# State-space stage of an adaLN network: merged dt weights, a new order of the small steps, softplus summed by TensorE

## The reference, cut to what matters

```
xz = u @ m_in_w.T ; xc, z = split(xz)                  # 256 channels each
xc = silu(causal_conv4(xc) + conv_b)
x_dbl = xc @ xproj_w.T                                  # 8 dt ranks, 16 B, 16 C
dt = softplus(x_dbl[:8] @ dt_w.T + dt_b)
h  = exp(dt * A) * h + dt * B * xc                      # scan over 512 tokens, 16 states
y  = (sum over states of h * C + xc * Dp) * silu(z)
out = y @ m_out_w.T
```

## Time and profile before

| | before |
|---|---|
| median of 3 runs | 2072.83 us |
| profiled execution, its own time | 2059.48 us |
| its span | 2057.8 us |
| mean granted TensorE clock | 0.837 |
| busy: TensorE, VectorE, ScalarE, GpSimd | 80%, 66%, 49%, 48% of the span |

### The profile page before, as it was taken

How to read it: one execution, slowest core, us unless ns; L and a number is a source line. 1 busy time by engine, 2 the same in 40 slices (tenths; PEclk the granted TensorE clock), 3 DMA queues, 4 the chain that set the end, 5 groups by cost and what they waited for, 6 DMA issues and landing times. The chain is left out here.

```text
span 2057.8 us, 23202 instructions
## 1 busy us (share of the span) xinstructions
PE 1652.5 (80%) x7221; PEld 730.4 (35%) x7221; DVE 1350.7 (66%) x1527; ACT 1003.5 (49%) x1638; POOL 995.8 (48%) x524
## 2 busy tenths in 40 slices
PE   7767788888888888875855957698888889879998
PEld 5221222222222222211454744354444445633333
DVE  3079999999999999999552123566565655384444
ACT  3566666676666776674122523154444445441111
POOL 1169999999999999998441153011111000040000
PEclk8878888888888888877957966599999989989999
DMA  3044344434443433333003221422233330100001
GB/s 140 2 104 104 92 103 103 103 93 103 103 103 95 101 90 88 89 87 91 16 30 103 82 67 50 116 59 56 49 77 79 79 79 4 46 0 0 0 0 41
DMA packets 78636, 145.41 MB, mean 71 GB/s; under 512 B 10214, under 2 KB 40782, under 8 KB 76854
## 3 DMA queue, kind: packets, MB, share of 16 engines
q1 hardware_dynamic: 75350, 134.98, 25.8%
q0 software_dynamic: 3216, 9.51, 1.4%
HBM read 87.27 MB, written 23.53 MB: 54 GB/s over the span
## 5 line engine op out<-in xcount | busy, mean ns | idle before, releaser
L574 POOL TENSOR_TENSOR PR<-H,CS 128x1024 f32<-128x1024 f32 x256 | 599.4, 2359 | 75.1 <-DVE H L550 52.8
L550 DVE TENSOR_TENSOR_SCAN H<-DA,X 128x1024 f32<-128x1024 f32 x192 | 431.1, 2273 | 0.0
L456 PE MATMUL psY<-PR,fold 128*64 128x512 f32 x1024 | 341.0, 766 | 4.9 <-POOL PR L574 4.9
L538 DVE TENSOR_TENSOR X<-DU,psB 128x1024 f32<-128x1024 f32 x192 | 235.8, 1228 | 72.9 <-DMA DU<-ab 56.8
L526 ACT ACTIVATE DA<-DT,negA 128x511 f32<-128x511 f32 x384 | 247.6, 709 | 7.3 <-DMA DT<-W 6.4
L1278 ACT ACTIVATE a_PT<-a_psS 128x512 f32<-128x512 f32 x320 | 181.3, 601 | 138.5 <-PE a_psS L1182 134.6
L1325 DVE TENSOR_REDUCE a_MX<-a_psM 128x1 f32<-128x384 f32 (+3 forms) x352 | 205.0, 635 | 47.0 <-PE a_psM L1197 45.5
L1196 PE MATMUL a_psM<-a_kst,a_qst 72*128 72x512 bf16 (+3 forms) x512 | 147.4, 336 | 28.0 <-DMA a_kst<-scratch_k 17.5
L550 DVE TENSOR_TENSOR_SCAN H<-X,XS 128x1024 f32<-128x1024 f32 x64 | 146.2, 2284 | 30.2 <-ACT X L526 30.2
L585 POOL TENSOR_TENSOR XS<-DU,BS 128x1024 f32<-128x1024 f32 x64 | 151.0, 2360 | 0.0
L436 PE MATMUL psB<-ST,sel 96*128 96x512 bf16 x128 | 60.8, 475 | 106.4 <-DVE X L538 106.4
(11 more groups left out here) (258 smaller groups left out, 2733.0 us busy)
## 6 DMA issues: line engine op xcount, KB each, us to landing
CS<-c_rows SPq DMA_DIRECT2D x128, 256.0 KB, 3.8
DT<-W SPq DMA_DIRECT2D x64, 256.0 KB, 4.3
DU<-ab SPq DMA_DIRECT2D x64, 256.0 KB, 4.4
BS<-c_rows SPq DMA_DIRECT2D x64, 256.0 KB, 5.3
scratch_q<-a_partsq SPq DMA_DIRECT2D x24, 384.0 KB, 3.4
a_qst<-scratch_q SPq DMA_DIRECT2D x8, 1152.0 KB
a_kst<-scratch_k SPq DMA_DIRECT2D x24, 384.0 KB
scratch_k<-a_partsk SPq DMA_DIRECT2D x8, 384.0 KB, 4.4
```

What stands on the lines that cost most here:

```text
L456: last = nc.tensor.matmul(psY[h * HP:(h + 1) * HP, n % 2 * T:(n % 2 + 1) * T], fold[:, :], chunk(PR[n % 4], h), start=False, stop=n >= NS - 2)
L538: nc.vector.tensor_tensor(both(X[s % 2][:, :]), DU[p][:, at:at + 2, :], psB[:, :].unsqueeze(1).to_broadcast([P, 2, T]), ALU.mult).then_inc ...
L550: nc.vector.tensor_tensor_scan(H[s % 4][:, :], decay, x, 0.0, ALU.mult, ALU.add).then_inc(scan_done, 1)
L574: nc.gpsimd.tensor_tensor(both(PR[s % 4][:, :]), both(H[s % 4][:, :]), CS[q % 2][:, s // 2 % 2, :].unsqueeze(1).to_broadcast([P, 2, T]), A ...
```

## The change

The dt weights are merged once, in the input stage: the 8 columns of the x-projection that give dt's ranks are multiplied by dt_w, so that dt is made straight from u (dtW, 128 rows, two chunks). To that end the input stage begins with two transposes, a VectorE copy and two products on TensorE, and a second VectorE copy. In the turn, d0 and d1 come first, then new steps s0 and s1 (the sum rl + ab by products with the identity, copied to rl by ScalarE), then xp, n1 and n2, and c0 to c1 and z0, z1 last. Exp and Ln become entries of the table (slots 5 and 6). GpSimd no longer adds, and multiplies by u in its slot 11. The queue sends DT ahead of the store to c_rows. In the prologue SiLU is made in two halves. In the attention stage the queue stores the parts of q and k before it sends the first half of the maxima. Context lines far from a change are left out.

```diff
...
+def dt_weights(W):
+
+    at = OFF1["wmod0"][0] + NCH * T
+    return W[:, at:at + NCH * NCH * P].rearrange("p (c m) -> p c m", c=NCH)
+
+
 def mamba_inputs_stage(nc, W, hT, XP, convW, diagD, sel, fold, nsel):
...
+    dtW = dt_weights(W)
...
         ps = [ctx.enter_context(nc.psum_tensor(f"xp_ps{i}", [P, T], F32)) for i in range(4)]
+        xprojT = ctx.enter_context(nc.sbuf_tensor("xprojT", [104, NCH * P], F32))
+        dt_ps = ctx.enter_context(nc.psum_tensor("dt_ps", [P, NCH * P], F32))
+        dtW_ps = ctx.enter_context(nc.psum_tensor("dtW_ps", [P, NCH, NCH * P], F32))
         sem = lambda name: ctx.enter_context(nc.semaphore(name))
-        xp_ps_ready, xp_done = sem("xp_ps_ready"), sem("xp_done")
+        xp_ps_ready, xp_done, dtW_step = sem("xp_ps_ready"), sem("xp_done"), sem("dtW_step")
         with nc.Block() as block:
+            @block.vector
+            def _(dve):
+                dve.wait_ge(dtW_step, 1)
+                nc.vector.tensor_copy(xprojT[:, :], dt_ps[0:104, :]).then_inc(dtW_step, 1)
+                dve.wait_ge(dtW_step, 3)
+                nc.vector.tensor_copy(dtW[:, :, :], dtW_ps[:, :, :])
+
             @block.tensor
             def _(pe):
+                for c in range(NCH):
+                    last = nc.tensor.transpose(dt_ps[0:104, c * P:(c + 1) * P], w("xproj")[:, c * 104:(c + 1) * 104], w("ident"))
+                last.then_inc(dtW_step, 1)
+                pe.wait_ge(dtW_step, 2)
+                for c in range(NCH):
+                    last = nc.tensor.matmul(dtW_ps[:, c, :], xprojT[96:104, c * P:(c + 1) * P], w("dt_w")[96:104, :], start=True, stop=True)
+                last.then_inc(dtW_step, 1)
                 with pe.Fori(0, B // 2) as i:
...
         UZ = [sb(f"UZ{i}", [P, 4 * T]) for i in range(2)]
-        xd = W[:, OFF1["wmod0"][0] + NCH * T:OFF1["wmod0"][0] + 3 * T]
+        xd = W[0:2 * NS, OFF1["conv_w"][0]:OFF1["conv_w"][0] + T]
+        dtW = dt_weights(W)
         ST = [sb(f"ST{i}", [96, T], BF16) for i in range(2)]
...
         ASIDE = (3, 7, 11, 15)
-        ORDER = ("mout", "xp", "n1", "n2", "d0", "d1", "c0", "c1", "z0", "z1")
-        FIRST = ("c0", "c1", "z0", "z1", "xp", "n1", "n2", "d0", "d1", "c0+", "c1+", "z0+", "z1+")
+        ORDER = ("mout", "d0", "d1", "s0", "s1", "xp", "n1", "n2", "c0", "c1", "z0", "z1")
+        FIRST = ("c0", "c1", "d0", "d1", "s0", "s1", "xp", "n1", "n2", "z0", "z1", "c0+", "c1+", "z0+", "z1+")
         BEFORE, EACH = len(FIRST), len(ORDER)
...
-        PE_AT = {3: ("mout",), 4: ("xp",), 5: ("n1",), 6: ("n2",), 7: ("d0",), 8: ("d1",),
-                 10: ("c0a",), 11: ("c0b",), 13: ("c1a",), 14: ("c1b",), 16: ("z0",), 17: ("z1",)}
-        ACT_AT = {3: ("silu", "mout"), 4: ("xp",), 5: ("n1",), 6: ("n2",), 7: ("d0",), 8: ("d1",), 12: ("c0",), 15: ("c1",), 16: ("z0",), 17: ("z1",)}
+        PE_AT = {3: ("mout",), 4: ("d0",), 5: ("d1",), 7: ("s0",), 8: ("s1",), 9: ("xp",), 10: ("n1",), 11: ("n2",),
+                 12: ("c0a",), 13: ("c0b",), 14: ("c1a",), 15: ("c1b",), 16: ("z0",), 17: ("z1",)}
+        ACT_AT = {3: ("silu", "mout"), 4: ("d0",), 5: ("d1", "exp"), 6: ("ln",), 7: ("s0",), 8: ("s1",), 9: ("xp",), 10: ("n1",), 11: ("n2",),
+                  13: ("c0",), 15: ("c1",), 16: ("z0",), 17: ("z1",)}
...
             elif k == "xp":
-                pe.wait_ge(silu_done, v + 1)
                 for c in range(NCH):
...
                 n = int(k[1])
-                last = nc.tensor.matmul(pp[:, :], w("dt_w")[96:104, n * P:(n + 1) * P], xd[96:104, :], start=True, stop=True)
+                if k == "d0":
+                    pe.wait_ge(silu_done, v + 2 if u is not None else 1)
+                if k == "s0":
+                    pe.wait_ge(softplus_step, 2 * v + 2)
+                for c in range(NCH):
+                    if k[0] == "d":
+                        last = nc.tensor.matmul(pp[:, :], dtW[:, c, n * P:(n + 1) * P], chunk(UZ[pv], c), start=c == 0, stop=c == NCH - 1)
+                    else:
+                        last = nc.tensor.matmul(pp[:, :], w("ident"), chunk((rl, ab)[c], n), start=c == 0, stop=c == NCH - 1)
             last.then_inc(pp_ready, 1)
...
-                act.wait_ge(pp_copied, EACH * u + BEFORE if u is not None else used(None, "z1") + 1)
-                if u is not None:
-                    act.wait_ge(fin_done, u + 1)
+                act.wait_ge(pp_copied, EACH * u + BEFORE)
+                act.wait_ge(fin_done, u + 1)
                 nc.scalar.activation(UZ[pv][:, :], pre[:, :], ACT.Silu).then_inc(silu_done, 1)
+                return
+            if k == "silu_u":
+
+                act.wait_ge(pp_copied, used(None, "c1") + 1)
+                nc.scalar.activation(UZ[0][:, 0:NCH * T], pre[:, 0:NCH * T], ACT.Silu).then_inc(silu_done, 1)
+                return
+            if k == "silu_z":
+
+                act.wait_ge(pp_copied, used(None, "z1") + 1)
+                nc.scalar.activation(UZ[0][:, NCH * T:], pre[:, NCH * T:], ACT.Silu).then_inc(silu_done, 1)
+                return
+            if k == "exp":
+                act.wait_ge(pp_copied, used(u, "d1") + 1)
+                nc.scalar.activation(ab[:, :], ab[:, :], ACT.Exp, scale=-1.0).then_inc(softplus_step, 1)
+                return
+            if k == "ln":
+                act.wait_ge(softplus_step, 2 * v + 1)
+                nc.scalar.activation(ab[:, :], ab[:, :], ACT.Ln, bias=1.0).then_inc(softplus_step, 1)
                 return
...
                 if u is not None or k.endswith("+"):
-                    act.wait_ge(silu_done, v + 1)
+                    act.wait_ge(silu_done, v + 2)
                 nc.scalar.activation(chunk(pre, n), pp[:, :], ACT.Identity, bias=w("conv_b")[:, n:n + 1]).then_inc(pp_copied, 1)
...
                 if u is not None or k.endswith("+"):
-                    act.wait_ge(silu_done, v + 1)
+                    act.wait_ge(silu_done, v + 2)
                 nc.scalar.activation(chunk(pre, 2 + int(k[1])), pp[:, :], ACT.Identity).then_inc(pp_copied, 1)
...
                 nc.scalar.copy(ST[pv][0:32, :], pp[0:32, :])
-                nc.scalar.copy(xd[0:104, :], pp[0:104, :]).then_inc(pp_copied, 1)
+                nc.scalar.copy(xd[:, :], pp[0:2 * NS, :]).then_inc(pp_copied, 1)
             elif k[0] == "n":
...
                 nc.scalar.copy(ST[pv][rows, :], pp[rows, :]).then_inc(pp_copied, 1)
+            elif k[0] == "s":
+                last = nc.scalar.copy(chunk(rl, int(k[1])), pp[:, :])
+                last.then_inc(pp_copied, 1)
             else:
...
                 nc.scalar.activation(chunk(rl, n), pp[:, :], ACT.Relu, bias=w("dt_b")[:, n:n + 1]).then_inc(pp_copied, 1)
-                if n == 1:
-                    act.wait_ge(pp_copied, used(u, "d1") + 1)
-                    nc.scalar.activation(ab[:, :], ab[:, :], ACT.Exp, scale=-1.0).then_inc(softplus_step, 1)
-                    act.wait_ge(softplus_step, 2 * v + 1)
-                    nc.scalar.activation(ab[:, :], ab[:, :], ACT.Ln, bias=1.0).then_inc(softplus_step, 1)
...
-        def pool_dt(pool, v, pv):
-            pool.wait_ge(softplus_step, 2 * v + 2)
-            nc.gpsimd.tensor_tensor(rl[:, :], rl[:, :], ab[:, :], ALU.add).then_inc(dtu_ready, 1)
-
-        def pool_du(pool, v, pv):
-            pool.wait_ge(dtu_ready, 2 * v + 1)
+        def pool_du(pool, u, v, pv):
+            pool.wait_ge(pp_copied, used(None if u is None else u, "s1") + 1)
             nc.gpsimd.tensor_tensor(ab[:, :], rl[:, :], UZ[pv][:, 0:NCH * T], ALU.mult).then_inc(dtu_ready, 1)
...
                     pool_state(pool, 16 * u + j, j - NS, u + 1, 1 - p)
-                if j == 9 and more:
-                    pool_dt(pool, u + 1, 1 - p)
-                if j == 10 and more:
-                    pool_du(pool, u + 1, 1 - p)
+                if j == 11 and more:
+                    pool_du(pool, u, u + 1, 1 - p)
...
-        def send_c(sp, v, pv, copied):
-
-            sp.wait_ge(pp_copied, copied)
-            sp.dma_start(c_rows[ds(v * 2 * NS, 2 * NS), :], xd[0:2 * NS, :]).then_inc(c_stored, 16)
-            sp.wait_ge(dtu_ready, 2 * v + 1)
+        def send_c(sp, v, pv, u):
+
+            sp.wait_ge(pp_copied, used(u, "s1") + 1)
             spread_halves(sp, rl, DT[pv], dt_loaded)
-            sp.wait_ge(dtu_ready, 2 * v + 2)
+            sp.wait_ge(pp_copied, used(u, "xp") + 1)
+            sp.dma_start(c_rows[ds(v * 2 * NS, 2 * NS), :], xd[:, :]).then_inc(c_stored, 16)
+            sp.wait_ge(dtu_ready, v + 1)
             spread_halves(sp, ab, DU[pv], du_loaded)
...
             def _(sp):
-                send_c(sp, 0, 0, used(None, "xp") + 1)
+                send_c(sp, 0, 0, None)
                 with sp.Fori(0, B - 1) as i:
                     for p in range(2):
-                        send_c(sp, 2 * i + p + 1, 1 - p, used(2 * i + p, "xp") + 1)
-                send_c(sp, UNITS - 1, 1, used(UNITS - 2, "xp") + 1)
+                        send_c(sp, 2 * i + p + 1, 1 - p, 2 * i + p)
```

(29 more changed lines are left out.)

## The result

| | before | after |
|---|---|---|
| median, this comparison | 2073.01 us (4 runs, 2069.49 to 2075.66) | 2126.17 us (4 runs, 2121.86 to 2130.96) |
| profiled execution, its own time | 2059.48 us | 2130.96 us |
| its span, mean granted TensorE clock | 2057.8 us, 0.837 | 2129.1 us, 0.883 |
| busy: TensorE, VectorE, ScalarE, GpSimd | 80%, 66%, 49%, 48% | 79%, 63%, 48%, 45% |

The ratio is 1.0258, 95% interval 1.0228 to 1.0288. The change makes the kernel **53.5 us (47 to 60) slower**. The forecast was 2127 us.

What follows compares the result with a forecast made beforehand. VectorE was taken to bound the state-space stage; +4.1 us a turn gives +61 over 15 turns, with +6.6 ahead of the first turn and -13 in attention +55 us, so 2127 us; range 2105 to 2145, 8 in 10 2090 to 2150.

Steps and rivals of the forecast that it cites:

- State 11's wait: State-space turn: VectorE's 2.04 us wait for ScalarE before the scan of state 11 goes, 28.6 us in 14 turns.
- DU: State-space turn: the later du product makes the next unit's first product wait 2.65 us for the DU transfer, 2.3 more.
- psB(10): State-space turn: TensorE's write for states 10 and 11 comes late behind s0, so product 10 waits 4.05 us more.
- E5: The end of scan 5 on VectorE, from which times in a turn are measured; product 10 was due at E5+9.2.
- psB(12): State-space turn: TensorE's write for state 12 comes 0.5 us late where it cost 0.34 a turn before: +0.1.
- Ahead of the first turn: Input stage +2 us for added transposes, copy and products, state-space prologue +4.6 for its new order; together +6.6 us.
- Attention: Parts stored before the maxima let the stack load start 2 us earlier, six times: -13 us, ends -25 and +6.
- Clock stays high: Rival: TensorE's clock stays high or recovers quickly and DU lands sooner; 2079 to 2095 us, chance 0.11.
- s0 not late: Rival: Ln ends before E5+5.8, psB(10) makes its window and a turn changes by nothing; 2066 us, chance 0.10.
- TensorE becomes the bound: Rival: TensorE stays at 1.2 GHz through s1 and the x-projection, +3 us a turn more; 2172 us, chance 0.07.
- The drain: Rival: a ScalarE table switch also costs the page's 1.38 us drain; +21 us, 2148 us, chance 0.02.
- Nothing: Rival: the moved steps only trade places in idle time and nothing comes of them; 2072.8 us, chance 0.03.

Runs made afterwards that it cites:

- e1: The kernel before, unchanged, run once more for a second profile: 2078.53 us.
- e12: The changed kernel, run once more: 2124.81 us, ratio 1.0248 to the kernel before.
- e4: The changed kernel with GpSimd's product with u back in slot 10: 2089.43 us, ratio 1.0055 to the kernel before.
- e8: The kernel before with only GpSimd's product with u moved one slot later, to 11: 2110.25 us, ratio 1.0155.
- e7: The changed kernel with three unread products on TensorE ahead of s0's wait for Ln: 2103.49 us, ratio 1.0103 to the kernel before.
- e9: e6 with unread products on TensorE, one ahead of the wait for YZ and three in slot 7: 2032.06 us, ratio 0.9795 to the kernel before.
- e5: The changed kernel with s0, s1, xp, n1 and n2 one slot later, s0 behind psB(10): 2088.63 us, ratio 1.0054 to the kernel before.
- e6: The changed kernel with the moves of e4 and e5 together: 2048.52 us, ratio 0.9825 to the kernel before.
- e10: e6 with the prologue's c1+ moved behind psB(2) and z1+ behind psB(4): 2035.98 us, ratio 0.9791 to the kernel before.
- e3: The kernel before with only attention's new queue order, parts stored ahead of the maxima: 2068.81 us, ratio 0.9958.
- e11: e10 with attention's maxima sent by GpSimd's queue instead of SyncE's: 2055.68 us, ratio 0.9912 to the kernel before.

## Why the prediction was right, point by point

The forecast was +55 us on the profile's scale and 2127 us on that of the median; measured are +53.5 us and 2126.17. Its direction and both of its new waits are shown by experiments. That the total agrees within 1 us is partly luck: the turns were put 11 us too high and attention's gain 4 us, and the measured 53.5 has an interval of 47 to 60. Between the spans of e1 and e12, the second profiles of the two kernels, it is 47.2 us.

- **State 11's wait goes** (-2.04): right, 28.6 us became 0.0. The YZ wait goes too, as forecast.
- **DU** (2.65 of wait): right in place, mechanism and size, 2.62 to 2.70. e4 and e8 show it alone, from both sides: -42 and +32 us.
- **psB(10)** (+4.05): right in place and mechanism, and 0.2 too large. Of the idle time ahead of s0 I had 5.2 us, it is 3.70 or 4.68; s0 takes 3.3 to 3.7 where I had 3.7. In the turn at 540 E5 is 551.94 (549.71 and one scan of 2.23). s0 starts at E5+7.4 where E5+7.6 was forecast, and product 10 at E5+13.0 where E5+13.3 was; it waits 3.87 us. In the other kind of turn products 6, 8 and 10 share 3.92. The end that I gave for a fast clock, 1.8, was met by 1.77 in e7; that for a slow one throughout, 4.8, was passed in one kind of e4's turns (5.12). The parts that I listed for Ln add up to 7.5 and not 7.6, and those of the two ends to 1.7 and 4.7, which changes nothing.
- **Products 6 and 8** (0.20 and 0.86): not forecast. I had said that TensorE has more time ahead of YZ, and used it to strike the YZ wait. I did not carry on: having more time there it sits idle 3.35 us, and in most turns mout and the D products behind it run slowly. e9 shows that this is the cause. It was covered in the changed kernel, where product 10 waits as much less, and it costs time only when that wait is out of the way or shorter, as in e5, e6 and e7.
- **psB(12)** 0.29 against 0.5 forecast.
- **The sum of a turn:** the waits are 6.87 us (0.20+0.86+2.86+0.29+2.66) against 3.04 before, +3.8 where +4.1 was forecast. The turn itself shows +3.4 (54.6 to 58.0); of the other 0.4, 0.2 are VectorE's busy time (50.75 us in the turn against 50.98), and 0.2 lie in gaps of the kernel before too short to have a row of their own, which I can't name. Over the turns the stage lost 49.7 us (53.2 between e1 and e12) instead of 61. This is the term that was mis-sized.
- **Ahead of the first turn:** input stage +2.9 (2.0 in e12) for +2, between the first transposition of the new group (51.31) and the input stage's first product (54.23). From c0 to product 4 it is +1.9 for +4.6. The wait behind c1+ is there, 5.28 us at product 2 and 2.46 at product 4, and e10 shows that it is worth 7.3; but product 0 came 5.7 us earlier after c0 (49.3 to 43.6 us), where I had counted on the 3.6 by which DT leaves earlier.
- **Attention** (-13, ends -25 and +6): -8.7 (-12.7 to -5.0) in e3. The exchange of one wait for another came as forecast: 21.7 us for the stack went, 14.5 for the maxima came. The size did not: I expected each loop to win 2 us, from 57.8 to 55.8, and they last 57.0 in the mean of five, from one store of the parts to the next (58.1 before, but 57.0 in e1).
- **Together:** by the stages of the two profiles +8.0 +49.7 -6.8 make +51. Of the 8.0, 2.9 and 1.9 are the change's. 1.1 lie ahead of it, and for 2.1 the input stage's products took longer: 16.1 us against 14.0 in before's profile. That is no part of the change, since they took 15.7 in e1 and 14.0 in e12.

**The rivals.** *Clock stays high:* it would have been the psB(10) wait of e7; it is not what happened, since s0 was slow, at least in part, in all 14 turns of the changed kernel. *s0 not late:* fallen by 443.81. I had put it at 2066; e5, in which s0 stands in nobody's way and DU is as in the changed kernel, took 2088.63 (ratio 1.0054), because the waits of products 6, 8 and 12 stay. *TensorE becomes the bound:* fallen; e5 and e6 do the same products, and one more slot of distance is enough. *The drain:* the start to start of 1.29 us around the table load leaves no room for it. The Trainium skill (ScalarE: Activation LUTs, What ACT_TABLE_LOAD costs) has 1.38 us more for a switch; the measurement decides. *Nothing:* fallen.

**What stays open.** e9 and e10 were not run together; by their parts that should give some 7 us more than e9, an estimate. How e11's time in attention divides between two causes is open, and so is why the stretch between state space and attention, which loads by index, varies by 20 us between executions.

## What to carry to other kernels

A step moved one slot on an in-order engine has to be priced by what stands behind it there: the softplus sums made product 10 wait up to 3.9 us a turn in front of the write of a single-buffered psB, and one slot later the turns were 2.2 us shorter, and the du product cost its whole 2.3 us because a transfer follows it. Where a new wait leaves TensorE idle for several us, count with the slow clock for at least part of the products behind the wait, look for every other place where the change makes it idle as well, and consider products that nobody reads ahead of the wait (here 24 us and 11 us less in the turns of the profiles). Before a difference of two profiles is explained, a second profile of the unchanged kernel shows how much of it is the change.

## What the runs showed of the hardware that I had not expected

- The same idle stretch led to either clock. Behind 3.35 us of idle time at YZ mout and the D products took about 5.6 us in 10 of 14 turns of after (6.8 in the first), and 3.9 (1.98+1.88) in the others. Behind 3.00 us in e6 psB took 0.61 in 4 turns and 0.39 in the 6 others. Behind 1.19 us in e9 and 0.93 in e7 the next products were fast.
- Nor was it the longer idle stretch that had the slow clock. In e6 mout and the D products were fast behind 2.64 to 2.73 us (4 turns) and in part slow behind 2.26 to 2.54 (the other 10), in e4 behind 2.26 us slow in 10 turns and fast in 4, and in e8 even 1.86 to 1.97 us of idle time were followed by slow ones in 4 turns (2.87 and 2.73 us).
- By when the full clock came back, the restart at s0 cost 3.9 or 5.1 us (e4). In e6 the turns last between 51.9 and 54.1 us; with unread products at both places (e9) 51.8 to 51.9.
- A small store on a queue of its own was no quicker past bulk stores than behind them on the same queue: from its issue to the load behind it 3.9 us in most turns of e11 and 5.1 in the one shown, on SyncE's queue 3.5 in most turns of after (1445.34 to 1448.81, below) and e10, and 5.2 and 5.1 in one each. Without bulk stores ahead of it it was 1.4 in the kernel before.

SyncE's queue of after, in order of time:

```profile
1445.34 1.13 SPq L1463 DMA_DIRECT2D m_scratch<-a_MTS  x1
1448.81 0.25 SPq L1465 DMA_DIRECT2D a_qst<-m_scratch  x1
```
